# First feed-forward layer of a macaron block: one plain 32-bit matmul in place of three rounded ones

## The reference, cut to what matters

```python
h = shift_token(x)
h = (h - mu) / jnp.sqrt(var + 1e-05) * lg + lb
h = h @ w1 + b1                      # 256 -> 2 * 682
a, g = jnp.split(h, 2, axis=-1)
h = a * jax.nn.gelu(g, approximate=False)
x = x + h @ w2 + b2                  # 682 -> 256
```

## Time and profile before

| | |
|---|---|
| median of 3 runs | 3195.17 us (3194.49 to 3196.07) |
| span of the profiled execution | 3193.4 us |
| instructions in it | 99022 |
| mean granted TensorE clock | 0.991 |
| TensorE busy | 3068.6 us, 96% |
| VectorE busy | 2350.6 us, 74% |
| ScalarE busy | 1729.0 us, 54% |
| GpSimd busy | 1622.9 us, 51% |

### The profile page before, as it was taken

One profiled execution on the slowest core, in us unless ns is written; L12 is line 12 of the kernel. 1 busy time (PEld: TensorE's weight loads), 2 busy tenths in 40 slices (PEclk: granted clock), 3 DMA queues, 4 the chain that ended last, 5 costly groups with the idle time before them and its releaser, 6 DMA issues.

```text
span 3193.4 us, 99022 instructions
## 1 busy us (share of the span) xinstructions
PE 3068.6 (96%) x35586; PEld 2681.3 (84%) x35586; DVE 2350.6 (74%) x6543; ACT 1729.0 (54%) x4532; POOL 1622.9 (51%) x1839
## 2 busy tenths in 40 slices
PE   6999999999999999999899999989999899999889
PEld 5888878878887888998788878878888788888778
DVE  6888767677776787777777767767777688777766
ACT  4767642266767224665667672237767622454445
POOL 7777730177776224333777761037777444317610
PEclk9999999999999999999999999999999999999999
DMA  4211121021111101000211112102111200100001
GB/s 135 67 45 44 37 81 33 23 63 40 36 40 39 42 20 43 11 10 21 58 40 36 40 39 76 30 26 66 37 39 34 72 21 13 27 0 1 1 14 40
DMA packets 178774, 122.82 MB, mean 38 GB/s; under 512 B 27533, under 2 KB 175337, under 8 KB 178025
## 3 DMA queue, kind: packets, MB, share of 16 engines
q1 hardware_dynamic: 177432, 117.77, 13.8%
q10 hardware_dynamic: 1104, 1.90, 0.2%
HBM read 48.29 MB, written 20.98 MB: 22 GB/s over the span
## 4 chain that ended last, share of the span: by engine, by line
PE 87%; DVE 6%; issue 3%; POOL 1%; ACT 1%; DMA 1%; SPq 0%; DVEq 0%; POOLq 0%; ACTq 0%
PE bank L347 15%; PE bank L348 13%; PE bank L349 13%; PE bank L511 8%; PE bank L480 6%; PE bank L452 3%; PE bank L732 2%; PE bank L731 2%; PE bank L730 2%; PE bank L724 2%; PE bank L725 2%; PE bank L489 2%; PE bank L676 2%; PE bank L675 2%; PE bank L490 2%
## 5 line engine op out<-in xcount | busy, mean ns | idle before, releaser
L2652 POOL TENSOR_TENSOR prob<-prob,rsum 128x384 f32<-128x384 f32 x512 | 416.2, 834 | 155.8 <-DVE rsum L1861 155.8
L1209 ACT ACTIVATE prob<-prob,nmax 128x192 f32<-128x192 f32 x1024 | 455.8, 454 | 2.2 <-DVE nmax L1854 2.2
L1401 ACT ACTIVATE gate<-bank,bias 128x512 f32<-128x512 f32 x192 | 132.4, 690 | 512.0 <-PE bank L349 511.9
L2639 POOL TENSOR_TENSOR rn<-ss,mhalf 128x16 f32<-128x16 f32 x128 | 375.9, 2937 | 10.7
L1854 DVE CUSTOM_DVE_ANT_0 prob<-bank,masks,rn 128x192 f32<-128x192 f32 x768 | 275.1, 414 | 100.1 <-PE bank L480 99.3
L2646 POOL TENSOR_TENSOR qk<-rot_t 128x512 f32<-128x512 f32 x256 | 331.9, 1297 | 23.3 <-DVE ss L1828 21.3
L347 PE MATMUL bank<-wqkv_hi,hT_hi 128*128 128x512 f32 x768 | 329.5, 429 | 14.7 <-DVE rot_t L1816 6.1
L2620 POOL TENSOR_TENSOR rstd<-meanvar,eps 128x4 f32<-128x4 f32 x48 | 12.4, 259 | 620.4 <-DVE meanvar L1786 620.4
L348 PE MATMUL bank<-wqkv_lo,hT_hi 128*128 128x512 f32 x768 | 303.0, 395 | 0.0
L349 PE MATMUL bank<-wqkv_hi,hT_lo 128*128 128x512 f32 x768 | 302.8, 394 | 0.0
L347 PE MATMUL bank<-gT_hi,w_hi 128*128 128x512 f32 x704 | 277.2, 394 | 2.6 <-issue 2.6
(11 more groups left out here) (292 smaller groups left out, 9831.1 us busy)
## 6 DMA issues: line engine op xcount, KB each, us to landing
Vlo<-V SPq DMA_DIRECT2D x256, 64.0 KB, 2.0
Vhi<-V SPq DMA_DIRECT2D x256, 64.0 KB, 2.0
H<-Y SPq DMA_DIRECT2D x128, 64.0 KB, 1.8
H<-ya SPq DMA_DIRECT2D x128, 64.0 KB, 1.8
yb<-Y SPq DMA_DIRECT2D x128, 64.0 KB, 1.6
HB<-Y SPq DMA_DIRECT2D x32, 256.0 KB, 2.8
HB<-yb SPq DMA_DIRECT2D x32, 256.0 KB, 3.1
raw<-in_L_ffn_wqkv SPq DMA_DIRECT2D x4, 1536.0 KB, 8.3
```

Of the source, the lines that this page charges most:

```text
L1209: ins = e.activation(pb, pb, ACT.Exp, bias=nm[r][:, x:x + 1], scale=-1.0, accum_out=sums[r][:, x:x + 1])
L2639: e.tensor_tensor(rn[u][:, :], ss[:, :], mhalf[:, :], ALU.pow).then_inc(s_plRN, 1)
L2652: e.tensor_tensor(pair, pair, rs[:, 2 * gi:2 * gi + 2].unsqueeze(2).to_broadcast([P, 2, KW]), ALU.mult).then_inc(s_plPN[gi], 1)
```

## The change

`w1` is kept whole in one tile `w1_full`, and the transposed input whole in `gT_full`, one tile for each parity of the group (`gT_even`, `gT_odd`). Each product, a pair of column block and k, is one plain 32-bit matmul of 512 columns. VectorE no longer splits the input (`tr`, `ffn_first`) and the weights (`w1_piece`) and clears one tail in place of two; a wait of it for GpSimd ahead of `ffn_first` goes with them. TensorE's transposes, its first piece and the start of a stage wait for ScalarE's semaphores (`s_acHI`, `s_prepA`) where they waited for VectorE's (`s_dvLO`, `s_prepV`). A placeholder `w1_rest` keeps the addresses of what lies behind.

```diff
-        w1_h, w1_l = sb("w1_hi", [P, KD, (2 * CH - 1) * P], F32R), sb("w1_lo", [P, KD, (2 * CH - 1) * P], F32R)
+        w1_full = sb("w1_full", [P, KD, (2 * CH - 1) * P])
+        gT_odd = sb("gT_odd", [P, KD, 512])
+        sb("w1_rest", [P, KD, (2 * CH - 1) * P - 512])
-        gF = [sb(f"gT_full{k}", [P, 512]) for k in range(KD)]
+        gT_full = [sb("gT_even", [P, KD, 512]), gT_odd]
...
# TensorE: tr, w1mm, piece, rest
-                    e.wait_ge(s_dvLO, 2 * G + OFF)
+                    if l0 or joined and isinstance(n, int) and n == 0:
+                        e.wait_ge(s_acHI, 2 * G + OFF)
+                    else:
+                        e.wait_ge(s_dvLO, 2 * (G - GRP * NRUN) + OFF)
...
-                            i = three(o, w1_h[w], w1_l[w], hi[:, k, :], lo[:, k, :], k == 0, k == KD - 1)
+                            i = e.matmul(o, w1_full[w], gT_full[par][:, k, :], start=k == 0, stop=k == KD - 1)
...
-                    if c == 0:
-                        e.wait_ge(s_dvLO, 2 * G + 2 + OFF)
+                    if c == 0 and l0:
+                        e.wait_ge(s_acHI, 2 * G + 2 + OFF)
+                    elif c == 0:
+                        e.wait_ge(s_dvLO, 2 * (G - GRP * NRUN) + 2 + OFF)
...
-                        e.wait_ge(s_prepV, prep['V'] + OFF)
+                        e.wait_ge(s_prepA, prep['A'] + OFF)
...
# ScalarE: w1_piece, tr
-                e.activation(w1_h[:, :, d0:d0 + n], W1[:, :, s0:s0 + n], ACT.Copy).then_inc(s_prepA, 1)
+                e.activation(w1_full[:, :, d0:d0 + n], W1[:, :, s0:s0 + n], ACT.Copy).then_inc(s_prepA, 1)
...
-                            e.activation(gF[k][:, :], bank[k][:, :], ACT.Identity, bias=vec[:, 4 + k:5 + k], scale=vec[:, k:k + 1]).then_inc(s_acHI, 1)
+                            e.activation(gT_full[par][:, k, :], bank[k][:, :], ACT.Identity, bias=vec[:, 4 + k:5 + k], scale=vec[:, k:k + 1]).then_inc(s_acHI, 1)
...
# VectorE: pass_A, w1_begin, w1_piece, tr, gated_group
                 w1_begin()
-                w1_piece(0)
                 slot(NT, 0)
-                w1_piece(1)
                 ffn_norm()
-                w1_piece(2)
-                w1_piece(3)
                 slot(NT + 1, 1)
-                e.wait_ge(s_plAD[0], NT * (run + 1) + OFF)
-                ffn_first()
                 slot(NT + 2, 2)
...
-                e.memset(w1_h[:, :, 2 * W1_MAIN:].bitcast(F32), 0.0).then_inc(s_prepV, 1)
-                e.memset(w1_l[:, :, 2 * W1_MAIN:].bitcast(F32), 0.0).then_inc(s_prepV, 1)
+                e.memset(w1_full[:, :, 2 * W1_MAIN:], 0.0).then_inc(s_prepV, 1)
...
-                e.tensor_tensor(w1_l[:, :, d0:d0 + n], W1[:, :, s0:s0 + n], w1_h[:, :, d0:d0 + n].bitcast(F32), ALU.subtract).then_inc(s_prepV, 1)
...
-                            e.tensor_copy(hi, full[:, :]).then_inc(s_dvGH, 1)
...
-                        if c == 3 and more:
-                            tr(n + 1, 1 - par)
```

More of the change, by code:

```diff
@@ L295, in build @@
         s_dvAG, s_plRV, s_dvXN, s_peTR, s_acHI, s_dvLO = sem("s_dvAG"), sem("s_plRV"), sem("s_dvXN"), sem("s_peTR"), sem("s_acHI"), sem("s_dvLO")
-        s_dvGH, s_peG, s_peA, s_acU, s_dvHD, s_xxHH = sem("s_dvGH"), sem("s_peG"), sem("s_peA"), sem("s_acU"), sem("s_dvHD"), sem("s_xxHH")
+        s_peG, s_peA, s_acU, s_dvHD, s_xxHH = sem("s_peG"), sem("s_peA"), sem("s_acU"), sem("s_dvHD"), sem("s_xxHH")
         s_dvHL, s_peW2, s_dvYB, s_peHF, s_sHB, s_mdvY = sem("s_dvHL"), sem("s_peW2"), sem("s_dvYB"), sem("s_peHF"), sem("s_sHB"), sem("s_mdvY")
@@ L315, in build @@
                       s_acOT, s_dvOT, s_peWO, s_dvY, s_plM0, s_dvST, s_dvAG, s_plRV, s_dvXN, s_peTR, s_acHI, s_dvLO,
-                      s_dvGH, s_peG, s_peA, s_acU, s_dvHD, s_xxHH, s_acHH, s_dvHL, s_peW2, s_dvYB, s_peHF, s_sHB, s_mdvY,
+                      s_peG, s_peA, s_acU, s_dvHD, s_xxHH, s_acHH, s_dvHL, s_peW2, s_dvYB, s_peHF, s_sHB, s_mdvY,
                       z_dvST, z_dvAG, z_plRV, z_acXN, z_peTR, z_acHT,
@@ L633, in prep_w1 @@
                 prep['A'] += 4
-                prep['V'] += 6
+                prep['V'] += 1
             def prep_w2():
@@ L1330, in w1_begin @@
                 e.wait_ge(s_raw, prep['raw'] + OFF)
-                prep['V'] += 2
+                prep['V'] += 1
                 need.update(prep)
@@ L1338, in w1_piece @@
                     e.wait_ge(s_prepV, need['V'] + OFF)
-                e.activation(w1_h[:, :, d0:d0 + n], W1[:, :, s0:s0 + n], ACT.Copy).then_inc(s_prepA, 1)
+                e.activation(w1_full[:, :, d0:d0 + n], W1[:, :, s0:s0 + n], ACT.Copy).then_inc(s_prepA, 1)
                 prep['A'] += 1
-                prep['V'] += 1
             def prep_w2(pas):
@@ L1787, in ffn_stats, with pass_A @@
                 i.then_inc(s_dvAG, 1)
-            def pass_A(run, finish, ffn_norm, ffn_first):
+            def pass_A(run, finish, ffn_norm):
                 R0 = NT * run
@@ L1998, in w1_begin @@
                 e.wait_ge(s_raw, prep['raw'] + OFF)
-                e.memset(w1_h[:, :, 2 * W1_MAIN:].bitcast(F32), 0.0).then_inc(s_prepV, 1)
-                e.memset(w1_l[:, :, 2 * W1_MAIN:].bitcast(F32), 0.0).then_inc(s_prepV, 1)
[L2001 to L2008, removed]
-                e.tensor_tensor(w1_l[:, :, d0:d0 + n], W1[:, :, s0:s0 + n], w1_h[:, :, d0:d0 + n].bitcast(F32), ALU.subtract).then_inc(s_prepV, 1)
+                e.memset(w1_full[:, :, 2 * W1_MAIN:], 0.0).then_inc(s_prepV, 1)
+                prep['A'] += 4
                 prep['V'] += 1
@@ L2051, in tr @@
                         full = bank[1 + 2 * k] if pas > NRUN and isinstance(n, int) and n == 0 else bank[k]
-                        if l0:
-                            full = gF[k]
-                            e.tensor_copy(hi, full[:, :]).then_inc(s_dvGH, 1)
-                            e.wait_ge(s_dvGH, 2 * G + k + 1 + OFF)
                         e.tensor_tensor(lo, full[:, :], hi.bitcast(F32), ALU.subtract).then_inc(s_dvLO, 1)
@@ L2207, in ffn @@
                 if l0:
-                    return norm, first, rest, finish
+                    return norm, rest, finish
                 if pas > NRUN:
@@ L2489, in vector_program @@
                     loads_B(l)
-                    norm, first, rest, next_finish = ffn(run, CH * GRP * run, True, next_loads=following, more=more, follow=first_steps if run == NRUN - 1 else None if more else linear_begin)
-                    pass_A(run, finish, norm, first)
+                    norm, rest, next_finish = ffn(run, CH * GRP * run, True, next_loads=following, more=more, follow=first_steps if run == NRUN - 1 else None if more else linear_begin)
+                    pass_A(run, finish, norm)
                     rest()
```

## The result

The changed kernel takes 3292.91 us (median of 4 runs, 3291.49 to 3296.20) against 3195.57 for the kernel before beside it (4 runs): a ratio of 1.0307, interval 1.0292 to 1.0322. That is 97 us slower, where 110 were forecast; 3305 stood as the time and 3290 to 3334 as the range. The profiled execution spans 3294.4 us and took 3296.2, the longest of the four; its span is 101.0 us longer than that of the kernel before.

What follows compares the result with a forecast made beforehand. TensorE was taken to bound the feed-forward stages; 3195.2 + 124 (plain products) - 1.3 (fourth-stage wait) - 10 (turns) - 3 (clock) = 3304.9, so 3305 us, range 3290 to 3334.

Steps and rivals of the forecast that it cites:

- What bounds the stages: Four feed-forward stages: TensorE busy 761.2 of 764.4 us, so its gains or losses count fully; work taken from VectorE is worth nothing.
- The plain product, two instructions of two cycles a column: First layer's 704 products: two records of 432 ns each, 0.864 us against 0.6875, so +124 us.
- the lower bound: Plain product by the slope of 0.81 ns a column: 421 ns a record, 593 us in all, +109 us.
- The upper bound: Plain product by simple scaling of line 1039's four records: 450 ns a record, 634 us in all, +150 us.
- The waits of the fourth stage: Fourth feed-forward stage: TensorE's 1.29 us wait for `Xn` of group 1 goes as products get longer, -1.3 us.
- The turn: Attention to feed-forward, four times: `rsum` comes earlier and idling before the stage goes, 2.4 to 2.5 us each, -10 us.
- the clock: In the four turns: TensorE idles less, so the granted clock falls less; half of 6 us, -3 us, ends 0 and 6.
- Weights bound the short matmuls: Rival: loading 128 weight columns sets the 110 ns record, so a 512-column record takes 0.229 us; 3019 us, 4 in 100.
- Overhead grows with the columns: Rival on the plain product: a record takes 450 ns, the term is +150, the time 3331 us; 12 in 100.
- The turns give nothing: Rival on the turns: GpSimd's chain or `Xn` is as late as before, the wait only renamed; 3319 us, 8 in 100.
- The change adds little: Rival on the stages: they had been waiting for something else, so a longer product fits in; no change, 1 in 100.

Runs made afterwards that it cites:

- The two experiments on the turn: Kernel before, `rsum` moved ahead of VectorE's clearings and subtraction: 3183.31 us against 3195.77; changed kernel, one subtraction put back ahead of `rsum`: 3301.43 us, 6.9 above its reference.

## Why the prediction was right, point by point

**What bounds the stages.** Right. Every ns of the longer product arrived: the first stage grew by 218.38 - 188.58 = 29.8 us, and 176 products by 0.858 - 0.6875 give 30.0. Put back, VectorE's work changed nothing.

**The plain product, two instructions of two cycles a column.** Right in its form, and the value chosen, 432 ns, was 3 ns too high: it carried the 5 ns a record of the 128-column rows to 512 columns, where 2.1 are found. 1408 x 3 ns is 4 us of the miss, about 4.5 by the unrounded steps. The true slope from 128 to 512 columns is (428.8 - 111.6) / 384 = 0.826 ns a column, so the 0.81 behind the lower bound was low. That is rounding: the 110 ns came from a chain's 0.44 us, and the starts of lines 1013 and 1039 in the same trace step at 111.1 ns, those of line 511 at 58.4 a pair, which gives (111.1 - 58.4) / 64 = 0.823. The upper bound, 450, scaled what does not scale. The run with 256 columns shows that nearly all is by column.

**The waits of the fourth stage.** Right in kind, too small: the one wait of 1.29 us was priced, but with the small ones there were 2.4 us in 6 waits, and what is left of the 4.1 below lies next to them, in matmuls that start late after an idle array (argued from their starts). The fourth stage grew by 222.53 - 196.86 = 25.7 us where the first grew by 29.8: -4.1, forecast -1.3.

**The turn.** Right in mechanism and too small, in good part by the clock. Forecast were -10 for VectorE's order and the split, and -3 for the clock. The first turn shrank by 4.5 us. The stretches from the last product of one stage to the first of the next, which hold the other three turns, shrank from 419.0, 687.2 and 419.6 us to 414.5, 683.6 and 415.6, so -16.4 us together. The -14.0 of the whole span is less mainly because this execution came to its first turn 2.9 us later than the one before (427.71 against 424.81); the profiled executions of all nine kernels come there between 424.4 and 429.3 us. With the medians in place of the profiled execution it is 97.3 - 115.0 = -17.7.

The parts of the first turn came as forecast: the longest wait fell by 1.9 us for 1.8, and the last block of transposes starts 431.46 - 427.71 = 3.8 us behind the start of the wait instead of 430.58 - 424.81 = 5.8; the 0.64 us went whole; and line 511's records took 1.3 us less at the higher clock. What was mis-sized is how often the clock stays up: half of the possible 6 us was taken, and it stayed up in three turns of four. At the forecast's own 1.6 us a turn that is some 4.8 us in place of 3, an estimate, so it makes about half of what the turns gave beyond the forecast; the rest was not followed up. The two experiments on the turn show the mechanism from both sides, one in each kernel.

**The rivals.** *Weights bound the short matmuls*: fell, by the steps of 429, 216 and 112 ns. The Trainium skill, in TensorE: Matmul & The Clock Gate, section LDWEIGHTS, gives a weight load the time of its columns divided by 1.2 GHz, an estimated 107 ns for 128. By the steps of 429 and 216 ns that is not what limits the plain matmul of 512 or 256 columns; whether it makes the 2.5 ns more at 128 was not tried. The run with one rounded matmul makes this rival's 3019 us doubtful for another reason (argued): with even less work on TensorE, though at a lower clock, the kernel took 3029.5. *Overhead grows with the columns*: fell, 2.1 ns. *The turns give nothing*: fell, -16.4 us. *The change adds little*: fell, 97 us.

**The sum.** 4.5 us of the product's step, 2.8 of the fourth stage and, by the medians, 4.7 of the turns make the 12 us by which 3305 was too high; by the profile's turns the last is 3.4. The executions of this kernel lie 4.7 us apart, those of others up to 11, so the last of these is the least certain.

## What to carry to other kernels

A plain 32-bit matmul cost four cycles a column here and a rounded one about one. So where TensorE sets the time, three rounded matmuls beat one plain one, 0.688 against 0.858 us at 512 columns, even though the plain one has fewer calls and spares another engine its splits. At 256 columns the rounded ones of the second layer step at 0.12 us, so three take 0.36 against 0.43; narrower ones were not compared. Read the price of an operand type from the distance between starts and from the number of records a call makes; durations hid it here: 1184 against 1176 ns. And look ahead of a stage at what stands in front of the small instruction that others wait for: moving a subtraction of 1.5 us and two clearings of 0.27 us behind a reciprocal in four turns gave the kernel before 12.5 us, some of it by the clock.

## What the runs showed of the hardware that was not expected

The rounded matmul of 512 columns steps at 229 ns, 16 above one cycle a column, while the plain one, of the same bytes, has only 2.1 above two. The overhead of a plain record at 128 columns is 4.9 ns, twice that at 256. And the granted clock is not a constant of a turn: in two profiled executions of the changed kernel, the fourth turn had a mean of 0.87 in one and 1.00 in the other, with the same order of work, and in the third it was the other way round, so a gain that hangs on it should be given with both ends. It goes with the spread of the times too: of nine executions of the kernel before on one chip, the fastest (3191.43 us) had a mean of 0.994 over the kernel, the slowest (3197.91) 0.991.
